# Attention eight tiles behind, P in three fp32r passes, four homes for the transposed a, and step 7 in another order

## What is computed

```
xn  = (x - mean) / sqrt(var + 1e-5)
q   = xn @ Wq.T + bq                     (only every 4th of 32 heads is used: 8 heads x 128)
s   = elu(q) + 1
a   = s @ M / (s @ z + 1e-6)             per head
att = repeat(a, 4 heads) @ Wo.T
out = x + att + xn @ (w * w_scale) + b
```

## Time and profile before

| | us |
|---|---|
| median of 3 runs (lowest to highest) | 241.03 (240.56 to 241.53) |
| the profiled execution | 240.47 |
| its span, first to last instruction | 238.7 |
| TensorE busy | 233.5 |
| VectorE busy | 170.8 |
| ScalarE busy | 120.3 |
| GpSimd busy | 100.4 |

### The profile page before, as it was taken

One profiled execution on the slowest core, in us unless ns is written; L12 is line 12 of the kernel. 1 busy time (PEld: TensorE's weight loads), 2 busy tenths in 40 slices (PEclk: granted clock), 3 DMA queues, 4 the chain that ended last, 5 costly groups with the idle time before them and its releaser, 6 DMA issues.

```text
span 238.7 us, 3385 instructions
## 1 busy us (share of the span) xinstructions
PE 233.5 (98%) x1029; PEld 186.9 (78%) x1029; DVE 170.8 (72%) x270; ACT 120.3 (50%) x276; POOL 100.4 (42%) x109
## 2 busy tenths in 40 slices
PE   7999999999999999999999999999999999999975
PEld 3688788888676788888888888888888888888865
DVE  2989999798688729696595876949475759853331
ACT  4846357763496525573744635264554946522110
POOL 1039437856335008282725242352405446666100
PEclk9999999999999999999999999999999999999999
DMA  7999999999762121626271827251213425776941
GB/s 222 396 414 414 345 251 257 221 205 218 157 248 51 47 52 50 174 60 166 58 210 50 211 54 208 53 135 48 89 50 94 97 89 132 180 203 151 210 179 47
DMA packets 24145, 38.76 MB, mean 162 GB/s; under 512 B 5440, under 2 KB 13376, under 8 KB 22976
## 3 DMA queue, kind: packets, MB, share of 16 engines
q1 hardware_dynamic: 19200, 26.36, 33.0%
q0 software_dynamic: 3680, 11.01, 24.1%
q10 hardware_dynamic: 1248, 1.18, 1.8%
HBM read 25.95 MB, written 4.19 MB: 126 GB/s over the span
## 4 chain that ended last, share of the span: by engine, by line
issue 42%; POOL 24%; DMA 15%; SPq 10%; DVE 3%; PE 3%; ACTq 1%; ACT 1%; POOLq 0%; DVEq 0%
DMA x<-in_WoT 13%; POOL e_and_sz L324 13%; SPq L226 6%; POOL xT L299 6%; POOL x L330 3%; POOL rstd L293 2%; DMA aT<-s 2%; SPq L210 1%; DVE aT_lo L669 1%; ACTq L473 1%; DVE den L648 1%; SPq L202 1%; SPq L207 1%; ACT aT_hi L466 1%; PE attn_ps L805 1%
## 5 line engine op out<-in xcount | busy, mean ns | idle before, releaser
L324 POOL TENSOR_TENSOR e_and_sz<-s,z_b 128x512 f32<-128x512 f32 x32 | 41.6, 1337 | 40.6 <-DVE den L648 40.6
L455 ACT ACTIVATE s<-s,rden 128x128 f32<-128x128 f32 x128 | 39.2, 389 | 37.0 <-DVE rden L652 37.0
L805 PE MATMUL attn_ps<-P_hi,aT_hi 128*128 128x512 f32 (+1 forms) x128 | 49.8, 389 | 1.3 <-DVE aT_lo L669 1.3
L807 PE MATMUL attn_ps<-P_hi,aT_lo 128*128 128x512 f32 (+1 forms) x128 | 49.1, 383 | 0.0
L806 PE MATMUL attn_ps<-P_lo,aT_hi 128*128 128x512 f32 (+1 forms) x128 | 48.9, 382 | 0.0
L805 PE MATMUL q_ps<-WqT_hi,xT_hi 128*128 128x512 f32 x104 | 41.6, 400 | 0.0
L807 PE MATMUL q_ps<-WqT_hi,xT_lo 128*128 128x512 f32 x104 | 40.5, 390 | 0.0
L806 PE MATMUL q_ps<-WqT_lo,xT_hi 128*128 128x512 f32 x104 | 40.5, 389 | 0.0
L299 POOL TENSOR_TENSOR xT<-xT,mean_b 128x512 f32<-128x512 f32 x13 | 18.9, 1452 | 38.0 <-ACT mean_b L404 38.0
L636 DVE SCALAR_TENSOR_TENSOR q_ps<-q_ps,rstd,bq_b 128x512 f32<-128x512 f32 x28 | 21.1, 754 | 18.9 <-PE q_ps L807 18.9
L805 PEld LDWEIGHTS attn_ps<-P_hi,aT_hi 128*128 128x128 f32 x128 | 24.1, 188 | 6.8 <-DVE aT_lo L669 1.8
(11 more groups left out here) (90 smaller groups left out, 364.9 us busy)
## 6 DMA issues: line engine op xcount, KB each, us to landing
x<-in_WoT POOLq DMA_DIRECT2D x6, 1024.0 KB, 11.2
x<-in_b POOLq DMA_DIRECT2D x16, 256.0 KB, 4.2
aT<-s SPq DMA_DIRECT2D x124, 32.0 KB, 1.9
out<-x SPq DMA_DIRECT2D x15, 256.0 KB, 2.8
x<-in_x SPq DMA_DIRECT2D x14, 256.0 KB, 4.7
xT<-in_xT SPq DMA_DIRECT2D x13, 256.0 KB, 4.4
MT<-s SPq DMA_DIRECT2D x96, 32.0 KB, 1.9
x<-in_WoT SPq DMA_DIRECT2D x2, 1024.0 KB, 13.9
```

The source lines that it names most:

```text
L324: nc.gpsimd.tensor_tensor(sz_eps[:, :, h * D // 2:(h + 1) * D // 2].rearrange("p g (j c) -> p j g c", j=2), by_quarter(sbuf_s[:, t % SRING ...
L455: last = nc.scalar.activation(a_g, a_g, ACT.Copy, scale=rden[:, t % 2, g:g + 1])
L805: nc.tensor.matmul(out, x_hi, w_hi, start=start, stop=False)
L807: return nc.tensor.matmul(out, x_lo, w_hi, start=False, stop=stop)
```

## The change

- **P**: M is split once (`copy_M_hi` on ScalarE, `split_M_lo` on VectorE, into the not yet used second buffer of aT_hi and aT_lo), each Wo_sum block by ScalarE (`copy_Wo_hi`) and by GpSimd (blocks 0 to 3) or VectorE (4 to 7), into the places where P_hi and P_lo of the same block come later. The eight products become `three_passes`.
- **Lag**: step t holds attention of t-8 instead of t-7, and eight tiles of attention follow after step 15. SP issues the moves of t-5 in step t and stores t-9.
- **Homes**: two more, made of the xT ring (its slots 0 and 1, and 2 and 3), take tiles 10 and 14, and 11 and 15. Tile 10's moves wait for xT_lo(13), 11's for xT_lo(15), 12's to 15's for the low half of the tile four before.
- **Shared moves**: tile 10's 16 are now 12 by SP and four by ScalarE; tile 11's are eight, four and four.
- **Order of step 7 and of what stands around it**, on all engines. P products 0 and 1 now follow both halves of q of tile 6. The denominators and a of tile 3 and the block transposes of tiles 1 and 2 come later, the split of xT(8) and the moments of 9 and 10 earlier.

```
-    FIRST_SHARED = T - 5
+    FIRST_SHARED = T - 6
     LEAD = 7
+    LAG = 8
...
+        def place(t):
+            return {T - 6: 2, T - 5: 3, T - 2: 2, T - 1: 3}.get(t, int(t >= 2 and t % 2 == 0))
...
+        def place_free(t):
+            if t in (T - 6, T - 5):
+                return xT_lo_ready, t + 5 + (t == T - 5)
+            return aT_lo_ready, 2 * t - (6 if t >= T - 4 else 2)
...
@@ SP
             spread_blocks(1)
-            spread_blocks(2)
             for t in range(LEAD, T):
...
-                spread_blocks(t - BEHIND - 1)
-                if t - LEAD >= 1:
-                    store(t - LEAD - 1)
-            for t in range(T - BEHIND - 1, T):
+                spread_blocks(t - BEHIND - 2)
+                if t - LAG >= 1:
+                    store(t - LAG - 1)
+            for t in range(T - BEHIND - 2, T):
                 spread_blocks(t)
-                if t < T - 2:
-                    store(t - BEHIND - 1)
-            for t in range(T - 2 * BEHIND, T - 1):
+                if T - BEHIND - 2 < t < T - 2:
+                    store(t - BEHIND - 2)
+            for t in range(T - 2 * BEHIND - 1, T - 1):
                 store(t)
@@ GpSimd
             center(7)
+            for g in range(GJ):
+                split_Wo_lo(g)
             times_z(3, 0)
             times_z(3, 1)
             add_b(0)
+            rstd_of(8)
+            center(8)
             times_z(4, 0)
             times_z(4, 1)
-            rstd_of(8)
-            center(8)
...
+                        if u == T - 2:
+                            spread_last_group(FIRST_SHARED + 1)
@@ ScalarE
             make_a(1)
+            copy_M_hi()
...
             copy_mean(7)
+            for g in range(GJ):
+                copy_Wo_hi(g)
             copy_P_hi(0)
             exp_of(6, 0)
             copy_P_hi(1)
             copy_xT_hi(7)
+            for g in range(GJ, G):
+                copy_Wo_hi(g)
             exp_of(6, 1)
             copy_P_hi(2)
+            copy_P_hi(3)
+            copy_mean(8)
+            copy_aT_hi(0)
+            copy_xT_hi(8)
             make_a(2)
-            copy_P_hi(3)
-            copy_aT_hi(0)
-            copy_mean(8)
             copy_P_hi(4)
-            copy_P_hi(5)
-            make_a(3)
             for t in range(LEAD, T):
+                if t == LEAD:
+                    copy_P_hi(5)
                 exp_of(t, 0)
-                if t + 1 < T:
+                if LAG < t < T - 1:
                     copy_xT_hi(t + 1)
+                exp_of(t, 1)
                 if t == LEAD:
                     copy_P_hi(6)
-                exp_of(t, 1)
-                if t == LEAD:
+                    copy_mean(t + 2)
+                    make_a(3)
                     copy_P_hi(7)
-                copy_aT_hi(t - LEAD + 1)
-                if t + 2 < T:
+                    copy_xT_hi(t + 2)
+                if t >= LAG:
+                    copy_aT_hi(t - LAG + 1)
+                if LEAD < t < T - 2:
                     copy_mean(t + 2)
+                if t >= T - 2:
+                    spread_group(FIRST_SHARED + t - T + 2)
...
-            spread_group(FIRST_SHARED)
-            copy_aT_hi(T - LEAD + 1)
+            copy_aT_hi(T - LAG + 1)
+            spread_group(FIRST_SHARED + 2)
+            copy_aT_hi(FIRST_SHARED)
             make_a(T - 2)
-            spread_group(FIRST_SHARED + 1)
-            copy_aT_hi(FIRST_SHARED)
+            copy_aT_hi(FIRST_SHARED + 1)
+            spread_group(FIRST_SHARED + 3)
             make_a(T - 1)
@@ VectorE
             make_s(5, 0)
+            split_M_lo()
+            make_s(5, 1)
             turn_blocks(1)
-            make_s(5, 1)
...
             add_bias(6, 1)
+            split_Wo_lo(4)
             moments(8)
             split_P_lo(2)
-            denominator(3)
+            split_Wo_lo(5)
+            split_Wo_lo(6)
             make_s(6, 1)
             split_P_lo(3)
+            split_Wo_lo(7)
             add_dense(6)
+            split_xT_lo(8)
+            split_aT_lo(0)
+            moments(9)
             split_P_lo(4)
+            split_P_lo(5)
+            add_bias(7, 0)
+            denominator(3)
             turn_blocks(2)
-            split_P_lo(5)
-            split_aT_lo(0)
+            add_bias(7, 1)
...
+                if t == LEAD:
+                    add_dense(t)
+                    split_P_lo(6)
+                    moments(10)
+                    turn_blocks(t - BEHIND - 1)
+                    split_P_lo(7)
+                    split_xT_lo(t + 2)
...
@@ TensorE
-                nc.tensor.matmul(attn_ps[g % 2][:], MT[:, g, :], Wo_sum[:, g, :], start=True, stop=True
-                                 ).then_inc(P_filled, 1)
+                three_passes(attn_ps[g % 2][:], MT_hi[:, g, :], MT_lo[:, g, :], Wo_hi[:, g, :], Wo_lo[:, g, :], True, True
+                             ).then_inc(P_filled, 1)
...
             product_q(6, 0)
+            product_q(6, 1)
             product_P(0)
             product_P(1)
-            product_q(6, 1)
+            product_dense(6)
             product_P(2)
             product_P(3)
-            product_dense(6)
-            product_P(4)
-            spread_mean(8)
             for t in range(LEAD, T):
                 product_q(t, 0)
                 if t == LEAD:
-                    product_P(5)
+                    spread_mean(t + 1)
+                    product_P(4)
                 product_q(t, 1)
                 if t == LEAD:
+                    product_P(5)
+                product_dense(t)
+                if t == LEAD:
                     product_P(6)
-                    product_P(7)
-                product_dense(t)
                 if t + 2 < T:
                     spread_mean(t + 2)
-                product_attn(t - LEAD)
+                if t == LEAD:
+                    product_P(7)
+                if t >= LAG:
+                    product_attn(t - LAG)
```

More of the change, by code:

```diff
@@ L86, in retrieval_and_dense @@
         Wo_sum = x[:, FIRST_LENT:, :]
+        MT_hi = aT_hi[:, 1, :, :]
+        MT_lo = aT_lo[:, 1, :, :]
+        Wo_hi = P_hi
+        Wo_lo = P_lo
         mean_weights = aT[:, 2, 0:P]
@@ L149, in retrieval_and_dense @@
         a_turned = sem("a_turned")
-        aT_in = [sem(f"aT_in{i}") for i in range(2)]
+        aT_in = [sem(f"aT_in{i}") for i in range(4)]
         aT_in_by_pool = [sem(f"aT_in_by_pool{t}") for t in range(FIRST_SHARED + 1, T)]
@@ L187, in aT_landed @@
         def aT_landed(t):
-            return 16 * sum(moves_of_rest(u) for u in range(t + 1) if in_MT(u) == in_MT(t))
+            return 16 * sum(moves_of_rest(u) for u in range(t + 1) if place(u) == place(t))
         def moves_of_rest(t):
@@ L227, in spread_blocks @@
                                      sbuf_s[i * 32:(i + 1) * 32, t % SRING, j * E // 4:(j + 1) * E // 4]
-                                     ).then_inc(aT_in[in_MT(t)], 16)
+                                     ).then_inc(aT_in[place(t)], 16)
             def store(t):
@@ L326, in times_z, with split_Wo_lo @@
                                         ).then_inc(sz_ready, 1)
+            def split_Wo_lo(g):
+                pool.wait_ge(Wo_hi_ready, g + 1)
+                nc.gpsimd.tensor_tensor(Wo_lo[:, g, :], Wo_sum[:, g, :], Wo_hi[:, g, :].bitcast(F32), ALU.subtract
+                                        ).then_inc(Wo_lo_by_pool, 1)
             def add_b(t):
@@ L391, in _ @@
             times_z(T - 1, 1)
-            for t in range(FIRST_SHARED + 1, T):
+            for t in range(FIRST_SHARED + 2, T):
                 spread_last_group(t)
@@ L458, in copy_aT_hi @@
             def copy_aT_hi(t):
-                act.wait_ge(aT_in[in_MT(t)], aT_landed(t))
+                act.wait_ge(aT_in[place(t)], aT_landed(t))
                 if t > FIRST_SHARED:
@@ L547, in _ @@
                         make_a(u)
[L548 to L549 removed]
+            copy_aT_hi(T - LAG + 1)
+            spread_group(FIRST_SHARED + 2)
+            copy_aT_hi(FIRST_SHARED)
             make_a(T - 2)
[L551 to L552 removed]
+            copy_aT_hi(FIRST_SHARED + 1)
+            spread_group(FIRST_SHARED + 3)
             make_a(T - 1)
[L554 to L556 removed]
+            for t in range(FIRST_SHARED + 2, T):
                 copy_aT_hi(t)
+                if t + 2 < T:
+                    spread_group(t + 2)
         @block.vector
@@ L623, in split_wd_lo, with split_M_lo, split_Wo_lo @@
                                         ).then_inc(wd_lo_ready, 1)
+            def split_M_lo():
+                dve.wait_ge(M_hi_ready, 1)
+                nc.vector.tensor_tensor(MT_lo, MT[:], MT_hi.bitcast(F32), ALU.subtract).then_inc(M_lo_ready, 1)
+            def split_Wo_lo(g):
+                dve.wait_ge(Wo_hi_ready, g + 1)
+                nc.vector.tensor_tensor(Wo_lo[:, g, :], Wo_sum[:, g, :], Wo_hi[:, g, :].bitcast(F32), ALU.subtract
+                                        ).then_inc(Wo_lo_by_dve, 1)
             def split_P_lo(g):
@@ L784, in _ @@
```

(10 more changed lines are left out.)

64 lines of the change are left out of this document (37 added, 27 removed).

## The result

| | before | after |
|---|---|---|
| median of 6 runs (lowest to highest), us | 241.16 (240.56 to 241.53) | 238.16 (237.95 to 238.70) |
| ratio, with its 95% interval | | 0.9884 (0.9863 to 0.9905) |
| profiled execution, its span | 240.47, 238.7 | 237.95, 236.1 |

The change makes the kernel 1.2% faster; the forecast was 238.6. The page of the kernel after: its span, each engine's busy time, and the chain of waits by engine.

A forecast was written before the change was run, and what follows sets the result against it. TensorE was taken to bound the kernel, with one hole before tile 15. Span 238.7 - 1.35 - 1.49 + 0.4 = 236.3; time 241.03 - 2.44 = 238.6 us, own range 237.7 to 239.8, widened to 237.6 and 240.6.

The forecast's parts named there:

- Bound: Whole run: TensorE, busy 98% of the span, sets the time; only fewer passes or smaller holes at the ends help.
- P in three passes: P products on TensorE: eight of 0.86 us become 24 passes of 0.23, saving 1.35 us.
- Stalls of step 7: TensorE waits in reordered step 7: P(6) late by 0.3, small slacks elsewhere; 0.4 us lost, bounds 0 and 1.6.
- The walk: Reordered step 7 from 57.03, with old durations: due and done times of each hand-over; P(4) slack 0.1, P(6) late 0.3.
- Splits of M and Wo: Before and in step 7: M's copy 1.0 and subtraction 1.2 us, Wo's copies and subtractions, all covered; cost 0.
- GpSimd beside VectorE: Wo splits at 58 to 65: a meeting costs VectorE up to 0.9 us; at most one on its chain, inside the bound.
- the slow rival: At 57 to 98, GpSimd meetings delay VectorE: 5.0 us stall, 243.2 us; decides from 4.0 us of stall; chance 0.06.
- Lag, homes and sharing: Tail: SP's last move out at 220 instead of 224.5, so tile 15's hole of 1.49 us closes with 2 us over.
- The range: Total time: forecast's own range 237.7 (no stall) to 239.8; the execution's basis, 237.6, added below and 240.6 above.

The follow-up runs named there:

- experiment 7: Changed kernel with one more VectorE operation (512-column reduction, 0.62 us) behind the dense add of tile 6 in step 7: 238.56 us, ratio 0.9897.
- experiment 8: Changed kernel with three added VectorE operations (1.86 us) behind the dense add of tile 6 in step 7: 239.74 us, ratio 0.9951.
- experiment 2: Kernel before with M and Wo split and P in three passes alone; lag 7, old order, two homes: 241.51 us, ratio 1.0018.
- experiment 11: Changed kernel with all eight low halves of Wo made by GpSimd, the second four behind its b load of tile 0: 238.67 us, ratio 0.9912.
- experiment 5: Changed kernel with the two old homes and the old sharing of moves; lag eight and three passes stay: 243.31 us, ratio 1.0112.
- experiment 3: Kernel before with four homes, tiles 12 and 13 in the xT ring; lag, P and sharing as before: 240.70 us, ratio 1.0001.
- experiment 4: Kernel before with the changed kernel's four homes and shared moves, at lag 7 with plain fp32 P: 240.02 us, ratio 0.9957.
- experiment 6: Changed kernel with the old sharing: SP issues all 16 moves of tile 10 and 12 of tile 11; four homes stay: 242.46 us, ratio 1.0081.

## Why the prediction was right

- **Bound.** Right: TensorE alone ended the run, and both gains are on it, passes and a hole.
- **P in three passes, -1.35.** Right in kind. A pair takes 1.36 instead of 1.72, 0.18 for each product and 1.44 for eight. Rounding a pass to 0.23 made it 0.17.
- **Stalls of step 7, +0.4.** The size was right, and one site more than forecast. P(6) lost 0.15, and 0.08 because the first pass behind a wait takes 0.31 instead of 0.23, where 0.3 was forecast; P(4), to which the walk gave 0.1 of slack, lost 0.17, since a hand-over from VectorE to TensorE took 0.15 and the walk had rounded it away. That is 0.40. The two terms leave 1.13 and not 1.44 - 0.40 = 1.04, so about 0.1 was gained elsewhere in the stretch and not followed up; 0.95 was forecast. The walk of xT_lo(7), P_lo(2), the dense add and P_lo(4) came out within 0.2 us (67.71 for 67.55, 70.88 for 70.7, 74.55 for 74.5, 77.9 for 78.0). Experiments 7 and 8 show that the chain to P_lo(4) is the binding one; experiment 2 shows what the stalls would be in the old order.
- **Splits of M and Wo, 0.** Right. M took 1.05 and 1.22 us for the 1.0 and 1.2 forecast (a ScalarE copy of 1024 columns was in the trace of before after all, wd_hi with 1.06); dense(8) and dense(9) found their adds made.
- **GpSimd beside VectorE.** Inside the bound and, as placed, nothing: no VectorE row of 58 to 63 is lengthened. The reason given was only partly right: VectorE didn't wait through the first splits but worked until 61.42, on a block transpose (1.24), a reduction (1.19), and the dense add (0.70) and bias add (0.75) that read PSUM; the one subtraction of two SBUF tiles nearby, M's at 55.82, was over before the splits began. Experiment 11 shows the slow rival's mechanism at work where the placement doesn't spare VectorE's chain, 1.05 for a meeting (0.9 in the forecast), but with one such meeting on the chain TensorE loses 0.7 there, far from the 4.0 from which it would decide.
- **Lag, homes and sharing, -1.49.** Right: the hole closed. SP's last move was forecast at 220 and came at 220.58, a of tile 15 turned at 208.3 and came at 207.48, tile 15 started at 227.59 for 227.6. The slack was sized too small, 2 for 3.8: the last moves had landed before 222.43, at most 1.9 us behind the last issue, and the forecast took over 4.2 from the tail of before. Why they land sooner isn't shown.
- **What the prediction didn't say** is how far the parts depend on each other. It summed them as if each stood alone. By the runs the passes alone bring nothing (ratio 1.0018), homes alone nothing (1.0001), homes and sharing a third of it (0.9957), the whole but the passes 0.9926, the whole 0.9884. With the lag, homes without the sharing (1.0081) or neither of them (1.0112) are slower than the kernel before. The total was right since the walk was made of the whole. Nor did it see how large a part that is left out can be: 4.3 us for the sharing, with a gain of 2.44 forecast for everything.
- **The range.** Its lower end, 237.7, goes by the profiled execution (240.47 - 2.84); from the median, as the forecast itself goes, no stall at all would be 238.2. The measured 238.16 stands there although there were stalls, since the medians differ by 3.0, while the ratio gives 2.8 and the spans 2.6. The account above explains 2.6; the other tenths are the spread of executions.
- **Open:** the 0.17 us scattered over other steps, what the lag brings without the new order of step 7, and where the executions of experiment 5 at full clock lost their time.

## What to carry to other kernels

Walk the changed order through the trace of before with the old durations, and keep due time and done time of every hand-over side by side: done times came out right to 0.2 us, and the two smallest slacks of the list, -0.3 and 0.1, were the two that stalled. A slack under the cost of a hand-over, 0.15 here, is none. Where a queue's issuing feeds the tail, look at three things together, when the target is free, when the source is ready and when the queue gets there: taking away one of them only shows the next (experiments 3, 4 and 6). A cut on the bounding engine that adds work to the engine behind it needs its order made anew before it pays (experiment 2).

## What the runs showed of the hardware that was not expected

- **The granted clock fell behind a long hole in two traces.** With a hole of 3.4 us in TensorE (209.33, experiment 5) the clock went to the 1.2 GHz level 1.3 us after the work went on, and stayed there for 3.4 us; with one of 2.4 us (226.44, experiment 6) 0.9 us after, for 3.4 us again. In the other traces, with holes of 0.3 to 1.8 us, it stayed at 1.00. The price was about 1.6 us in each of the two. What sets it off is not shown: four of seven executions of experiment 6 kept 1.00, and five executions of the kernel before, whose traced execution has one hole of 1.3 us and kept 1.00, had a mean clock of 0.993, as these two do, and took 242.8 to 243.8 us.
- **The issue time of a move isn't constant.** SP's moves of tiles 14 and 15 take 0.70 us each in the changed kernel (16 in 11.22), 0.62 for tile 12 in experiment 3 (8 in 4.98), and 0.76 in experiment 6 (16 in 12.20). What it depends on isn't shown. Company on the other queues alone isn't it: in the changed kernel SP's eight moves of tile 11 took 4.97 (from 192.67) while ScalarE (192.85 to 195.38) and GpSimd (194.06 to 196.08) issued four each.
- **One meeting of two engines** more than doubled a VectorE subtraction, 0.68 to 1.73 (experiment 11), while GpSimd's four subtractions took 5.50 instead of 5.06.
